# VectorE makes graph messages two units ahead of TensorE's marks in most stages, and adds window sums one unit later

## The chip, the cores and the metric

One core of a Trainium2 chip runs the whole program. The metric is the device time of one execution in microseconds (us). Engines are named as the profile names them: PE is TensorE (PEld its weight loads), DVE is VectorE, ACT is ScalarE, POOL is GpSimd, SP is SyncE.

## The reference, cut to what matters

A graph with 3125 nodes of 256 features and 53125 edges (sorted by destination) goes through two relational graph layers. Beside them the same nodes go through four layers of linear attention and feed-forward, and both results enter a small mixture-of-experts head:

```python
def _mgcn_conv(x, edge_index, edge_type, rel, W_in, W_out, W_loop, b, n):
    m = x[src] * rel[edge_type]
    m = concat([m[:half] @ W_in, m[half:] @ W_out])
    agg = segment_sum(m * norm[dst][:, None], dst)
    return tanh(agg + x @ W_loop + b)
h = emb + res * _mgcn_conv(emb, ..., rel1, ...)
h = h + res * _mgcn_conv(h, ..., rel2, ...)
gnn = h @ mu_w + mu_b
for i in range(4):                       # the mixer, beside it
    x = x + linear_attention(layernorm(x))
    x = x + gelu(layernorm(x) @ W1[i] + b1[i]) @ W2[i] + b2[i]
out = r + experts(layernorm(r))          # r = x_in + gnn + mixer
```

## The kernel before, in words

**The edge work.** Edges are cut into steps of 128; a graph layer has 416 steps. Two steps are a *unit* (`UNIT = 2`), so a graph layer has 208 units, and unit numbers here run from 0 to 415 over both layers. Eight steps are a *window* (`WIN = 8`), so a window is four units (`UW = 4`). For each unit

- POOL gathers the source rows into `xg` (L956, one indirect DMA per step) and, in the first graph layer only, the relation rows of both layers into `rg` (L903, one per step). `xg` has room for 16 steps, that is eight units, so the gather of unit u waits until PE has done unit u-8.
- DVE makes the unit's one-hot matrices (`hot`, L1045) and the messages `xg * rg` (L1054). `hot` has room for eight steps (`HOTS = 8`), so DVE waits before L1045 until PE has done unit u-4. Before L1054 it waits for the unit's gathers (`s_edge`).
- PE multiplies one-hot by messages into a PSUM bank, eight steps (a window) into one of two banks (L2628). PE waits for `s_msg` of the unit, and at the first unit of a window for `s_acc`, which tells that both sums of the window two back have been added.
- DVE adds the window's bank into `acc` twice, for the destination tile and for the next (L1033), each time weighted by `in_tile`. The row number of `acc` is read into a register by `row_numbers` (a `value_load`).

In the second graph layer the relation rows come back from HBM by SP in blocks, so POOL has only the `xg` gathers.

**The order of the work.** Every engine's program is written out by hand. The mixer is cut into stages: a front, then for each layer 0 to 3 a joint (`joint`, the end of the attention) and five feed-forward groups (`iteration`, group (layer, gi)) of five tiles each. A table gives each stage a number of steps: 32 for the front, 14, 14, 14 and 36 for the joints, and (20, 26, 24, 24, 24), (20, 24, 24, 24, 22), (18, 24, 68, 48, 54), (58, 58, 58, 56, 48) for the groups. So group (0,1) begins with unit 33, (0,2) with unit 46, (0,3) with unit 58 and (0,4) with unit 70. Units 0 to 207 end in group (2,2), whose last 20 units run among the tiles of the graph layer's dense update (`dense`). The second graph layer is units 208 to 415, groups (2,3) to (3,4).

Within a stage, `marks` says by which unit each engine has come at each point of the mixer work. PE's program runs `upto(mark)` and then its mixer work. DVE's program has the same marks, but `Edges.stage(at, ahead)` lets it run `ahead` units further at each of them: `upto(k)` makes units while `done < base + k + ahead`, and `one(most)` makes one such unit. `units_ahead` gives that number for the groups: 0 in group (0,0) and in group (2,3), 1 in all others. Joints have `min(lay, 1)`: 0 in joint 0, 1 in the others. The front has 0.

**What stands behind a unit on DVE.** DVE works strictly in program order. In a group with the attention front of the next layer in it, the order after `upto(up0)` is: `f.stats`, which is the layernorm statistics of five rows (L509), `one(up1)`, the means and variances (L516), `one(up1)`, an inverse square root of ten small instructions (L486 to L505) with a third `one(up1)` in it, and then `f.norm(0)` and `f.norm(1)` (L1107), which make the rows that PE transposes next (L545, `f.turn(0)`). Group (0,1) has marks up0 = 2, up1 = 4 and down0 = 5. Further on in a group come `add_ffn` (L1227), `n.add_attention` (L1174), `k_max` (L1114), `n.norm` (L1209) and the softmax work (L1119 to L1160), with `upto` calls between them.

**Where adds stand.** With k the unit within its graph layer, `unit` reads the row numbers of window k//4 - 1 at the start of a unit with k % 4 == 0, and after the message of a unit with k % 4 == 2 or 3 it adds window k//4 - 1 for the first or second time.

Of the kernel before, what the change touches and what calls it, by code (L numbers as in the profile page):

```python
# [45 lines left out]
def build(nc, io, out):  # L46
# [14 lines left out]
    at_joint, at_group, steps = {}, {}, sum(STEPS_FRONT)  # L61
# [9 lines left out]
    RU, UW, BU = RING // UNIT, WIN // UNIT, BLOCK // UNIT  # L71
# [54 lines left out]
    with ExitStack() as ctx:  # L126
# [524 lines left out]
        def dense_before(lay, gi):  # L651
            return (lay, gi) == (DENSE_LAYER, DENSE_GROUP)

        def units_ahead(lay, gi):

            return 0 if (lay, gi) == (0, 0) or dense_before(lay, gi) else 1

        def dense_behind(lay, gi):
            return dense_before(lay, gi + 1)
# [314 lines left out]
        def _(dve):  # L974
# [36 lines left out]
            class Edges:  # L1011
# [24 lines left out]
                def unit(self):  # L1036
                    k, g = self.done, self.g
                    self.done += 1
                    if k % UW == 0 and k:
                        self.row_numbers(k // UW - 1)  # L1040
                    at = k * UNIT
                    s = at % RING
                    hs = at % HOTS
                    dve.wait_ge(s_seg, g * UNITS + (k + 1 + RU - HOTS // UNIT))
                    dve.tensor_tensor(hot[:, hs:hs + UNIT, :], iota_t[:, :].unsqueeze(1).broadcast_to([EP, UNIT, T]),  # L1045
                                      key_tab[:, at:at + UNIT].unsqueeze(2).broadcast_to([EP, UNIT, T]), ALU.is_equal)
                    m, r = xg[:, s:s + UNIT, 0:D], rg[:, s:s + UNIT, 0:D]
                    if g == 0:
                        dve.wait_ge(s_edge[k % RU], (k // RU + 1) * (2 * 16 * UNIT))
                    else:  # L1050
                        dve.wait_ge(s_edge[k % RU], (k // RU + 1 + 2 * (STEPS2 // RING)) * (16 * UNIT))
                        dve.wait_ge(s_r2ld[at // BLOCK % len(s_r2ld)], (at // (2 * RING) + 1) * 16)
                        r = rg2[:, at % (2 * RING):at % (2 * RING) + UNIT, :]
                    dve.tensor_tensor(m, m, r, ALU.mult).then_inc(s_msg, 1)  # L1054
                    if k % UW in (2, 3) and k > UW:
                        self.add(k // UW - 1, k % UW - 2)

                def added(self):

# [958 lines left out]
                front_tiles(fronts[ga], fronts[ga - 1], None if is_last(ga) else fronts[ga + 1], front_marks(ga), upto, one)  # L2018
                at += STEPS_FRONT[ga]
            for lay in range(L):  # L2020
                joint_rest = joint(lay, *edges.stage(at_joint[lay], min(lay, 1)))
                for gi in range(NG):
                    if dense_before(lay, gi):
                        edges = Edges(1)

                    def begin():
                        if lay == L - 1 and gi >= NG - LAST_EARLY:
                            last_norm(gi - (NG - LAST_EARLY))

                    def early():  # L2030

                        if (lay, gi) == (L - 1, NG - 1):
                            edges.flush()

                    def aside(s):
                        if lay == L - 1:
                            dense_beside(gi * (2 * GT) + s)
                            if is_last(gi) and s == GT:
                                logits(0)
                                shift_logits(0)  # L2040
                    if (lay, gi) == (L - 1, 0):
                        general(1, any_unsorted())
                        self_split.read()
                        sums_scaled(0)
                        gate_order()
                    iteration(lay, gi, *edges.stage(at_group[lay, gi], units_ahead(lay, gi)), begin, early, joint_rest, aside)
# [1341 lines left out]
```

## Time and profile before

| | us |
|---|---|
| runs, device time | 1940.79, 1942.41, 1944.38 |
| median | 1942.41 |
| the profiled execution's own time | 1944.52 |
| its span (first to last instruction) | 1942.8 |
| PE busy / DVE busy / POOL busy | 1822.1 / 1248.2 / 1327.5 |

An engine's busy time is the time in which it executes. Idle time before an instruction is put down to what ended it: `<-DMA rg` is the landing of a gather, `<-PE ps_seg` a matmul, `issue` a time in which the engine waited for nothing that the profile shows. The mean granted TensorE clock was 0.991.

### The profile page before, as it was taken

How to read it: one execution, taken by the hardware profiler on the slowest of the kernel's cores; microseconds unless marked ns; L12 is line 12 of the kernel's file. 1: busy time of each engine (PE TensorE's matmuls, PEld its weight loads, DVE VectorE, ACT ScalarE, POOL GpSimd, SP SyncE). 2: the span in 40 equal slices, each digit the busy share in tenths (PEclk: the TensorE clock that was granted, in tenths of full speed). 3: DMA queues.
4: the chain of work that ended last, by engine and by line, in shares of the span. 5: the costliest groups of instructions: out<-in, count | busy, mean ns of one | idle time of the engine just before them, and what ended most of it. 6: DMA issues, size and time to landing. Idle time of an engine off the chain costs nothing.

```text
span 1942.8 us, 28973 instructions
## 1 busy us (share of the span) xinstructions
PE 1822.1 (94%) x9176; PEld 1505.0 (77%) x9176; DVE 1248.2 (64%) x3345; ACT 634.8 (33%) x1552; POOL 1327.5 (68%) x1326
## 2 busy tenths in 40 slices
PE   3889999999899999999999789998999999999999
PEld 1557777887688888768887667886788888888998
DVE  6786465674855576486465555959765666664766
ACT  4452233343323343332333222323122212223443
POOL 6777777777777777777777757777777777770000
PEclk9999999999999999999999999999999999999999
DMA  9568766667866666687777856566767666661000
GB/s 274 178 199 256 205 191 203 187 202 217 250 206 204 194 199 193 208 250 215 206 209 212 263 177 237 181 208 212 236 183 221 201 200 199 190 188 24 15 28 28
DMA packets 194575, 371.44 MB, mean 191 GB/s; under 512 B 37993, under 2 KB 126095, under 8 KB 194430
## 3 DMA queue, kind: packets, MB, share of 16 engines
q0 software_dynamic: 77632, 223.91, 40.4%
q1 hardware_dynamic: 92228, 126.68, 19.8%
q10 hardware_dynamic: 24570, 19.04, 3.4%
q8 instruction: 76, 1.25, 0.3%
q14 instruction: 69, 0.57, 0.1%
HBM read 305.39 MB, written 64.95 MB: 191 GB/s over the span
## 4 chain that ended last, share of the span: by engine, by line
PE 76%; DVE 8%; POOL 5%; issue 4%; DMA 4%; SPq 2%; ACT 1%; DVEq 0%; POOLq 0%; ACTq 0%
PE ps_down L2764 15%; PE ps_hid L2752 15%; PE ps_seg L2628 14%; PE ps_kv L2661 5%; PE ps_x L2716 3%; PE ps_x L545 3%; POOL xg L956 3%; PE ps_kv L3081 2%; PE ps_hid L3228 2%; POOL rg L903 2%; DMA qT_all<-xn_rows 2%; DVE xg L1054 1%; PE ps_hid L2681 1%; PE ps_x L3081 1%; PE ps_hid L3219 1%
## 5 line engine op out<-in xcount | busy, mean ns | idle before, releaser
L956 POOL DMA_INDIRECT xg<-h_rows,idx_tab x416 | 434.3, 1044 | 141.6 <-issue 114.8
L956 POOL DMA_INDIRECT xg<-xn_rows,idx_tab x416 | 434.2, 1044 | 130.9 <-issue 122.2
L903 POOL DMA_INDIRECT rg<-relation_rows,idx_tab x416 | 419.1, 1007 | 133.6 <-issue 126.4
L2628 PE MATMUL ps_seg<-xg,hot 128*125 128x257 f32 x1664 | 417.3, 383 | 18.3 <-DVE xg L1054 18.0
L2752 PE MATMUL ps_hid<-hT,wff 128*128 128x250 f32 (+1 forms) x1920 | 368.1, 340 | 0.2
L2628 PEld LDWEIGHTS ps_seg<-xg,hot 128*125 128x125 f32 x1664 | 307.1, 189 | 74.1 <-DVE xg L1054 15.9
L2764 PE MATMUL ps_down<-wff,gT 128*125 128x256 f32 x1600 | 362.8, 380 | 0.0
L2752 PEld LDWEIGHTS ps_hid<-hT,wff 128*128 128x128 f32 x1920 | 312.7, 189 | 36.9 <-issue 6.8
L2764 PEld LDWEIGHTS ps_down<-wff,gT 128*125 128x125 f32 x1600 | 294.8, 188 | 41.3
L1054 DVE TENSOR_TENSOR xg<-xg,rg 128x512 f32<-128x512 f32 x416 | 285.5, 686 | 61.0 <-DMA rg<-relation_rows,idx_tab 46.1
L2203 ACT ACTIVATE gT<-ps_hid,b1p 128x250 f32<-128x250 f32 (+1 forms) x480 | 177.9, 433 | 292.3 <-PE ps_hid L2752 292.1
L1045 DVE TENSOR_TENSOR hot<-iota_t,key_tab 128x250 f32<-128x250 f32 x416 | 171.2, 411 | 36.8 <-PE ps_seg L2628 26.4
L2661 PE MATMUL ps_kv<-wqkv,hTa 128*125 128x512 f32 x240 | 112.9, 593 | 0.0
L1033 DVE SCALAR_TENSOR_TENSOR acc<-ps_seg,in_tile,acc 125x257 f32 x208 | 99.7, 479 | 17.4 <-PE ps_seg L2628 16.7
L2114 ACT ACTIVATE kx<-ps_kv 125x256 f32<-125x256 f32 x72 | 27.7, 384 | 237.4 <-PE ps_kv L2661 228.5
L1227 DVE TENSOR_TENSOR xres<-xres,ps_down 125x256 f32<-125x256 f32 x100 | 40.0, 416 | 93.9 <-PE ps_down L2764 89.1
L1174 DVE TENSOR_TENSOR xres<-xres,ps_x 125x256 f32<-125x256 f32 x80 | 30.8, 417 | 103.8 <-PE ps_x L2716 103.8
L2189 ACT ACTIVATE hT<-ps_x,ln2p 128x250 f32<-128x250 f32 (+1 forms) x120 | 56.0, 522 | 96.4 <-PE ps_x L545 94.6
L1114 DVE TENSOR_TENSOR kmax<-kmax,kx 125x256 f32<-125x256 f32 x54 | 22.9, 425 | 84.3 <-ACT kx L2114 83.7
L2716 PE MATMUL ps_x<-cwo,qT_all 128*125 128x256 f32 x320 | 76.8, 379 | 0.0
L2661 PEld LDWEIGHTS ps_kv<-wqkv,hTa 128*125 128x125 f32 x240 | 44.7, 187 | 33.2 <-issue 29.0
L2716 PEld LDWEIGHTS ps_x<-cwo,qT_all 128*125 128x125 f32 x320 | 59.8, 187 | 9.3
(373 smaller groups left out, 2390.1 us busy)
## 6 DMA issues: line engine op xcount, KB each, us to landing
second_relation_rows<-rg SPq DMA_DIRECT2D x104, 512.0 KB, 4.0
rg<-second_relation_rows SPq DMA_DIRECT2D x104, 512.0 KB, 4.0
wff<-L_mix_W ACTq DMA_DIRECT2D x8, 1024.0 KB
rg<-relation_rows,idx_tab POOLq DMA_INDIRECT x416, 3.7
xg<-xn_rows,idx_tab POOLq DMA_INDIRECT x416, 3.5
xg<-h_rows,idx_tab POOLq DMA_INDIRECT x416, 3.7
qT_all<-xn_rows SPq DMA_DIRECT2D x25, 112.0 KB
h_rows<-qT_all SPq DMA_DIRECT2D x25, 112.0 KB
```

What stands on the lines that cost most here:

```text
L903: pool.indirect_dma_start(rg[:, k, :], None, rel_d, bass.IndirectOffsetOnAxis(ap=idx_tab[:, step, 1:2], axis=0))\
L956: pool.indirect_dma_start(xg[:, k, 0:D], None, rows, bass.IndirectOffsetOnAxis(ap=idx_tab[:, step, 0:1], axis=0))\
L1033: dve.scalar_tensor_tensor(a, ps_seg[w % 2][0:T, 0:AW], in_tile[:, ds(w, 1), m], a, ALU.mult, ALU.add).then_inc(s_acc, 1)
L1045: dve.tensor_tensor(hot[:, hs:hs + UNIT, :], iota_t[:, :].unsqueeze(1).broadcast_to([EP, UNIT, T]), key_tab[:, at:at + UNIT].unsqueeze(2). ...
L1054: dve.tensor_tensor(m, m, r, ALU.mult).then_inc(s_msg, 1)
L2203: ins = act.activation(out, hidden, ACT.Gelu, bias=b1p[:, ff:ff + 1])
L2628: ins = pe.matmul(ps_seg[u // UW % 2][0:T, 0:AW], hot[:, s % HOTS, :], xg[:, s % RING, :], start=s % WIN == 0, stop=s % WIN == WIN - 1)
L2661: ins = pe.matmul(ps_kv[0:T, :], hTa[:, j % 2, c, :], wqkv[:, c, 0:2 * D], start=c == 0, stop=c == KC - 1)
L2716: ins = pe.matmul(ps_b[j % 2][0:T, :], q[:, c * T:(c + 1) * T], cwo[:, c, :], start=c == 0, stop=c == KC - 1)
L2752: ins = pe.matmul(hidden, w1[:, c, ff * P:(ff + 1) * P], hT[:, a:z, c, :], start=c == 0, stop=c == KC - 1)
L2764: ins = pe.matmul(ps_down[j % 2][0:T, :], gT[:, j % 2, f, :], w2[:, f, :], start=f == 0, stop=f == FC - 1)
L3081: ins = pe.matmul(out_rows, sums(k), weights[k // KC](k % KC), start=k == 0, stop=k == n - 1)
```

## The change

`units_ahead` gives 2 in place of 1, and joints 1 to 3 get 2 in place of 1. Group (0,0), group (2,3), joint 0 and the front stay at 0. In `unit` the reading of row numbers goes behind the message of the unit. The first add of a window follows the message of the unit with k % 4 == 3 (before: 2), and the second follows that of the unit with k % 4 == 0 of the next window (before: 3), ahead of the new row numbers. The last unit of a graph layer does both adds of the window before its own.

```diff
         def units_ahead(lay, gi):
 
-            return 0 if (lay, gi) == (0, 0) or dense_before(lay, gi) else 1
+            return 0 if (lay, gi) == (0, 0) or dense_before(lay, gi) else 2
...
                 def unit(self):
                     k, g = self.done, self.g
                     self.done += 1
-                    if k % UW == 0 and k:
-                        self.row_numbers(k // UW - 1)
                     at = k * UNIT
...
                     dve.tensor_tensor(m, m, r, ALU.mult).then_inc(s_msg, 1)
-                    if k % UW in (2, 3) and k > UW:
-                        self.add(k // UW - 1, k % UW - 2)
+                    if k % UW == 3 and k > UW:
+                        self.add(k // UW - 1, 0)
+                        if k == UNITS - 1:
+                            self.add(k // UW - 1, 1)
+                    if k % UW == 0 and k > UW:
+                        self.add(k // UW - 2, 1)
+                    if k % UW == 0 and k:
+                        self.row_numbers(k // UW - 1)
...
-                joint_rest = joint(lay, *edges.stage(at_joint[lay], min(lay, 1)))
+                joint_rest = joint(lay, *edges.stage(at_joint[lay], 2 * min(lay, 1)))
```

## Rows read from the trace of the kernel before

**Rows 1.** The page: busy us (share of the span) xinstructions.
```profile
PE 1822.1 (94%) x9176; PEld 1505.0 (77%) x9176; DVE 1248.2 (64%) x3345; ACT 634.8 (33%) x1552; POOL 1327.5 (68%) x1326
```
**Rows 2.** Windows: stretch, length, busy us and count by engine, clock, DMA share, GB/s.
```profile
221.00:295.00 74.00, 68.73 (x321) 55.23 (x320) 43.77 (x114) 23.72 (x57) 57.16 (x56) 0.98 0.68 199
...
362.00:428.00 66.00, 65.67 (x319) 53.88 (x318) 40.84 (x109) 25.14 (x58) 50.77 (x51) 1.00 0.67 197
```
**Rows 3.** Waits, whole span: who waited <- for whom: us, times, longest.
```profile
DVE xg L1054 <- DMA rg<-relation_rows,idx_tab: 46.1, 23, 4.5
...
DVE hot L1045 <- PE ps_seg L2628: 26.4, 20, 3.1
...
PE ps_seg L2628 <- DVE xg L1054: 18.0, 16, 2.8
```
**Rows 4.** Waits of PE, 221 to 533 us (groups (0,1) to joint 1).
```profile
PE ps_seg L2628 <- DVE xg L1054: 2.8, 1, 2.8
```
**Rows 5.** Waits of PE, 1230 to 1767 us (second graph layer).
```profile
PE ps_seg L2628 <- DVE xg L1054: 4.9, 5, 1.6
```
**Rows 6.** Waits of POOL, 171 to 498 us (layer 0's groups).
```profile
POOL xg L956 <- PE ps_seg L2628: 0.9, 3, 0.3
```
**Rows 7.** Waits of DVE, 221 to 498 us.
```profile
DVE xg L1054 <- DMA rg<-relation_rows,idx_tab: 44.1, 19, 4.5
```
**Rows 8.** Waits of DVE, 533 to 1050 us (layers 1 and 2), the first of the list.
```profile
DVE kmax L1114 <- ACT kx L2114: 84.8, 20, 7.8
```
**Rows 9.** Timeline, group (0,1): start us, us, instruction, count, [idle before <-releaser].
```profile
230.81 0.69 DVE L1054 TENSOR_TENSOR xg<-xg,rg 128x512 f32<-128x512 f32 x1 [2.46 <-DMA rg<-relation_rows,idx_tab]
...
231.65 1.89 PE L2628 MATMUL ps_seg<-xg,hot 128*125 128x257 f32 x4 [2.77 <-DVE xg L1054]
...
235.93 0.69 DVE L1054 TENSOR_TENSOR xg<-xg,rg 128x512 f32<-128x512 f32 x1 [3.77 <-DMA rg<-relation_rows,idx_tab]
...
238.57 0.75 DVE L1107 TENSOR_SCALAR kx<-xres,mv,rstd 125x256 f32<-125x256 f32 x2
...
239.13 0.41 PE L545 MATMUL ps_x<-ident,kx 125*128 125x125 f32 x2 [1.24 <-DVE kx L1107]
...
242.12 0.69 DVE L1054 TENSOR_TENSOR xg<-xg,rg 128x512 f32<-128x512 f32 x1 [2.47 <-DMA rg<-relation_rows,idx_tab]
```
**Rows 10.** Timeline, late in group (0,3).
```profile
408.60 1.88 POOL L903 DMA_INDIRECT rg<-relation_rows,idx_tab  x1 [0.30 <-issue]
...
412.03 0.95 POOL L903 DMA_INDIRECT rg<-relation_rows,idx_tab  x1 [0.30 <-issue]
...
414.41 0.73 DVE L1209 TENSOR_SCALAR xh<-xres,mv,rstd 125x256 f32<-125x256 f32 x2
...
415.33 0.59 PE L545 MATMUL ps_x<-ident,xh 125*128 125x125 f32 x4
```
**Rows 11.** Timeline, start of group (3,0).
```profile
1376.24 1.13 PE L2628 MATMUL ps_seg<-xg,hot 128*125 128x257 f32 x4 [1.40 <-DVE xg L1054]
...
1389.69 2.07 PE L2628 MATMUL ps_seg<-xg,hot 128*125 128x257 f32 x8 [1.59 <-DVE xg L1054]
```
**Rows 12.** The page's groups: line, operation, count | busy us, mean ns | idle before, releaser.
```profile
L1033 DVE SCALAR_TENSOR_TENSOR acc<-ps_seg,in_tile,acc 125x257 f32 x208 | 99.7, 479 | 17.4 <-PE ps_seg L2628 16.7
```
**Rows 13.** Line 1045's answer: DVE sat idle before it (us, times) until:
```profile
  issue: 7.0, 15
```
**Rows 14.** Timeline of DVE, front, ahead of unit 9.
```profile
100.22 0.42 DVE L1119 TENSOR_REDUCE ktop<-ps_hid 128x2 f32<-128x250 f32 x1 [0.35 <-PE ps_hid L545]
```
**Rows 15.** The page's DMA issues: out<-in, queue, count, us to landing.
```profile
rg<-relation_rows,idx_tab POOLq DMA_INDIRECT x416, 3.7
```
**Rows 16.** Timeline, dense update: unit 207's last gather, unit 206's message, PE later.
```profile
1134.29 0.95 POOL L903 DMA_INDIRECT rg<-relation_rows,idx_tab  x1 [0.30 <-issue]
...
1134.89 0.69 DVE L1054 TENSOR_TENSOR xg<-xg,rg 128x512 f32<-128x512 f32 x1
...
1143.83 0.68 PE L545 MATMUL ps_hid<-ident,qT_all 125*128 125x125 f32 x2 [2.68 <-DMA qT_all<-xn_rows]
```

## The prediction, made before the changed kernel was run

> **What bounds the kernel now.** I began with the page's busy times: PE 94%, POOL 68%, DVE 64% [rows 1]. PE is the bound unless a stage says otherwise. The table of windows says it stage by stage: group (0,3) keeps PE busy 65.67 of 66 us, while the 74 us of group (0,1) have 5.3 us without PE [rows 2]. Then the list of waits: over the whole span PE waits 18.0 us for messages, DVE waits 46.1 us for relation gathers and 26.4 us for a free one-hot slot [rows 3]. So the change can give back some of 18.0 us, and it touches two waits of DVE that are larger. Last, timelines at the places where these waits sit.
>
> Where are the 18.0 us? The front, at 0 ahead before and after, is outside the reach of the new lead. Layer 0's groups and joint 1 hold 2.8 us, in one wait [rows 4]. The second graph layer from 1230 us on holds 4.9 us in five waits [rows 5]. Layers 1 and 2 hold none in their groups. The rest lies in stages that stay at 0.
>
> Where are the gather waits? Of the 46.1 us, 44.1 lie between 221 and 498 us [rows 7]. There POOL is paced by itself: the gaps between its gathers are 0.3 us, nearly all of issue [rows 10], and only 0.9 us in all, three times 0.3, came right after PE's release of a slot [rows 6]. In group (0,3) it issued 51 gathers in 66 us, busy 50.77 us with some 15 us of such gaps [rows 2]. A unit of the first graph layer is four gathers, so it takes about 5.2 us, and a unit of PE takes 66/12 = 5.5 us. Gathers that begin late stay late. In layers 1 and 2 DVE's list of waits begins with 84.8 us for ACT [rows 8] and has no gather in its first seven entries: POOL has caught up.
>
> **The change part by part.** No instruction is added or removed: 416 one-hots, 416 messages and 208 adds stay. No DMA is moved in POOL's or SP's program. What moves is the place in DVE's program at which it waits for a gather or a slot.
>
> *The lead removes PE's waits for messages.* Where PE waits on a message whose gather had long landed, one more unit of lead covers it. That holds for 1376.24 (1.40 us) and 1389.69 (1.59 us) [rows 11] and for three smaller ones, together 4.9 us [rows 5]. I take all of it: **-4.9 us**. Ends: 0, if what is next late on DVE takes each place, and -4.9. The 2.8 us of layer 0 are not among them: the message at 230.81 that PE awaited at 231.65 had itself just waited for its gather [rows 9], and a lead does not make a gather land.
>
> *The lead adds DVE waits for gathers in layer 0, and what stands behind them is due.* The place is the start of group (0,1), where the lead goes from 0 to 2. Before, with 1, `upto(up0)` ends with unit 35, the two `one(up1)` make units 36 and 37 (230.81 and 235.93), both held by their gathers, and then come the inverse square root and the rows `kx` at 238.57, for which PE already waited 1.24 us at 239.13 [rows 9]. With 2, `upto(up0)` ends with unit 36 and the two `one(up1)` make 37 and 38. The message of unit 38 started at 242.12, held by its gather [rows 9], and POOL sends it no sooner. So the last message ahead of `kx` starts at 242.12 in place of 235.93, and `kx` and PE's transpose, which has nothing else to do in its order, come 242.12 - 235.93 = **+6.2 us** later. Ends: +6.2, and 0 if that gather lands 6 us earlier or the lag of that moment is gone; nothing excludes one to two more, see below.
>
> *Does it repeat in (0,2) to (0,4)?* There the rows `xh` at 414.41 are read by PE at 415.33 [rows 10], so a DVE delay of more than about 0.5 us just before would stop PE again, and the DVE waits of 44.1 us over 19 units [rows 7] say that gathers land shortly before DVE wants them. But PE, once 6.2 us later, finds POOL 6.2 us further on, which is more than the 5.5 us of one unit that the new lead asks for. So the loss pays for the lead once: I take 0 more. Ends: 0, and, if each of the three groups paid one more gather wait of the mean size, 3 x 44.1/19 = +7 [rows 7].
>
> *Adds and row numbers in stages at 0 ahead* (front, joint 0, groups (0,0) and (2,3)). PE needs the second add of a window and the message of the same unit; before, the add was done a unit earlier, in idle time of DVE. Now it stands between the unit with k % 4 == 0 and DVE's next work. In the front DVE comes from unit 8 to unit 9 with one idle piece, 0.35 us at 100.22 [rows 14], and the add (0.48 us [rows 12]) and the row numbers (7.0/15 = 0.47 us where they showed as idle time [rows 13]) now fall into that stretch: about 0.95 - 0.35 = +0.6 us each for units 9 and 13. The rest (row numbers no longer ahead of a message) is worth up to -0.4 a window. I take **+1**, ends -1 and +3. In the stages at 2 ahead the adds keep their place relative to PE's marks, so they cost 0.
>
> *The dense update.* Unit 207's message moves into the place of unit 206's, at 1134.89, but its last gather was issued at 1134.29 [rows 16] and lands some 3.7 us later [rows 15], at 1138.0. So DVE stands some 3.1 us in a tile and saves a message and a one-hot in the next. DVE's update feeds the stores and loads of rows, for which PE waits anyway (2.68 us at 1143.83) [rows 16], and part of the 3.1 us is DVE's own idle time in a tile. **+1**, ends 0 and +3.
>
> *The one-hot slots in layer 3.* With a lead of 2 the one-hot of unit u, which waits for PE's unit u-4, is asked for at PE's mark u-2 in place of u-1, so bursts of units end in longer DVE waits. They are 26.4 us in 20 waits now, up to 3.1 us [rows 3], and each may grow by the time of one PE unit, about 1.1 us [rows 11], and by more where other matmuls lie between. DVE is ahead of PE just then, which hides most of it. **+1.5**, ends 0 and +6 (a quarter of the 20 grown waits). Group (2,4), where POOL is again close, gets **+0.5**, ends 0 and +3.
>
> The sum: -4.9 + 6.2 + 1 + 1 + 1.5 + 0.5 = **+5.3 us**. Against the profiled execution's own time of 1944.5 us (span 1942.8) that is 1949.8. This execution lay 2.1 us over the median of 1942.4, so I forecast a median of 1942.4 + 5.3, rounded down because two small terms may be hidden: 1947.5 us.
>
> *A rule that bears on this.* A gather instruction at 408.60, beside two back-to-back units of DVE, took 1.88 us, one at 412.03 took 0.95 us [rows 10]. The Trainium skill, in "GPSIMD Engine Reference", section 1, Specifications, says that POOL's SBUF interface is shared with VectorE and contended when a DVE instruction has two SBUF inputs; the trace agrees, with the 0.93 us between these rows. By that rule the extra unit ahead of the waited-for gather would make +6.2 into up to +7.1; without it, it stays +6.2.
>
> **The rivals.**
>
> *Faster: the lead only covers.* The mechanism is DVE's backlog at the stage starts of the second graph layer (1376.24, 1389.69) [rows 11], and the gathers of layer 0 come early enough that unit 38 isn't waited for. It decides if unit 38's gather lands by the time that DVE had finished unit 37, 236.6 us. For it: runs differ by 3.6 us, and 221 to 295 us is where POOL's lag is decided. Against it: three messages in a row waited 2.5 to 3.8 us for their gathers [rows 9]. The time: -4.9 and the +1 of the adds, and nothing for the rest, 1942.4 - 3.9 = 1938.5 us. The Trainium skill, in "Trainium Kernel Development and Optimization", section Best Practices, advises to double-buffer so that DMA and compute overlap, and a deeper lead is that; by it alone the time would be this one.
>
> *Same: the two cancel.* PE's 6.2 us in group (0,1) shrink to about 4, because the gather wait at 231.65 and the one for `kx` overlap differently, and the 4.9 us are given back. 1942.4 us, from 1939 to 1945. For it: group (0,1) has only 5.3 us without PE now, so its gathers are not far behind. Against it: nothing of PE's work can be drawn ahead of its transpose.
>
> *Slower by more: every group of layer 0 pays.* PE doesn't fall behind POOL for good, because DVE's own waits hold the adds and the next units. Then -4.9 + 6.2 + 7 for the three groups, 1 + 1 + 0.5 as above and 3 for layer 3 make +13.8: 1956.2 us. For it: the slack of about 0.5 us at 414.41 [rows 10]. Against it: POOL in this stretch waits for no slot of PE's [rows 6], so any delay of PE widens POOL's lead.
>
> *The change does nothing there*: DVE already makes each message when its gather lands, so two ahead is one ahead in layer 0. This is true for messages and is why no gain is booked there; it is false for what stands behind them.
>
> **How the numbers follow.** Forecast 0.50, faster rival 0.21, same 0.19, slower by more 0.10. A change of under 0.2% (3.9 us) can't be told from none here. The forecast's own range is +1 to +9 us; of its 0.50 I put 0.40 above 3.9 us and 0.10 below. So slower is 0.40 + 0.10 = 0.50, same is 0.10 + 0.19 = 0.29, faster 0.21 (the faster rival reaches past -3.9 us if most of 4.9 us comes). The range: 1938.0 (the faster rival's time, a little extended; half of that rival lies beyond) to 1954.0 (+11.6, short of the last rival).
>
> **What would show it.** Right: in group (0,1) PE's transpose of `kx` waits about 7 us (1.24 + 6.2) behind a message held by a gather; DVE's waits for relation gathers in (0,2) to (0,4) stay near what they are, with PE's groups still about 66 us; the five waits of PE in the second graph layer go from 4.9 us to under 1; units 9 and 13 in the front wait some 0.6 us longer. Wrong: a group (0,1) that is no longer than 74 us, waits of PE for `xh` or `ktop` in (0,2) to (0,4), or a layer 3 with new waits of PE behind DVE's one-hot waits.

## The result: 1960.2 us, 0.98% slower, and the profile after

The changed kernel takes 1960.16 us (median of 4 runs, 1955.09 to 1964.88), the kernel before beside it 1942.74 us (1940.79 to 1944.38, 4 runs): ratio 1.0098, 95% interval 1.008 to 1.0116 (the plain quotient of the two medians is 1.0090; for all runs below, too, the ratio given is that of the comparison with its interval). I had forecast 1947.5 us with a range to 1954.0. The sign was right, the size was not, and the time lies outside the range. The profiled execution after is the shortest of its four: 1955.09 us, span 1953.4. Against the span before (1942.8) it shows 10.6 us of a loss that is 17.4 us between the medians.

The page of the changed kernel, its first row, against [rows 1]: nobody has more to do.

```profile
PE 1824.2 (93%) x9176; PEld 1506.7 (77%) x9176; DVE 1246.1 (64%) x3345; ACT 635.9 (33%) x1552; POOL 1319.4 (68%) x1326
```

The list of waits of the changed kernel over the whole span (who waited <- for whom: us, times, longest) answers to [rows 3]. Line 1043 is the one-hot (1045 before), 1052 the message (1054 before), 1786 is `mu_added`, the addition of a product to a row in the dense update of layer 3 (1782 before), and 3085 TensorE's next product, which takes that bank.

```profile
DVE hot L1043 <- PE ps_seg L2632: 63.3, 41, 3.6
...
DVE xg L1052 <- DMA xg<-h_rows,idx_tab: 24.4, 20, 4.4
...
DVE xg L1052 <- DMA rg<-relation_rows,idx_tab: 15.3, 8, 4.4
PE ps_seg L2632 <- DVE xg L1052: 8.4, 9, 1.8
PE ps_kv L3085 <- DVE xres L1786: 8.0, 7, 2.5
```

The same wait for `mu_added` in the kernel before:

```profile
PE ps_kv L3081 <- DVE xres L1782: 0.7, 2, 0.4
```

Three things are to be seen. DVE's waits for a one-hot slot went from 26.4 to 63.3 us. PE's waits for messages fell from 18.0 to 8.4 us, which is what a lead does. And a wait of PE that was 0.7 us in two places before, for `mu_added`, is now 8.0 us in seven.

Where the time went, by stages. I took from each timeline the start of the first window matmul of each stage; the columns are the stage's length in us; the dense update is counted from unit 189 to unit 208. (z1, z2 and x9 are experiments of below.)

| stage | before | after | z1 | x9 | z2 |
|---|---|---|---|---|---|
| front, joint 0, group (0,0) | 165.4 | 165.8 | 166.0 | 166.8 | 165.0 |
| group (0,1) | 74.6 | 80.3 | 70.5 | 74.1 | 69.4 |
| groups (0,2) to (0,4) | 202.4 | 200.5 | 199.1 | 200.1 | 200.2 |
| joint 1, layers 1 and 2 up to the dense update | 567.3 | 568.2 | 567.4 | 565.8 | 565.3 |
| dense update | 105.6 | 101.2 | 105.3 | 103.1 | 103.0 |
| group (2,3) | 77.6 | 77.9 | 79.3 | 77.6 | 77.9 |
| group (2,4) | 79.5 | 82.3 | 82.7 | 80.4 | 79.6 |
| joint 3 | 45.9 | 46.1 | 47.8 | 44.4 | 45.0 |
| layer 3 | 392.5 | 399.5 | 400.1 | 413.7 | 393.5 |
| the rest | 176.5 | 176.4 | 176.3 | 176.3 | 176.2 |

The first graph layer (first five rows) ends 0.5 us later than before: in this pair of executions what was lost in group (0,1) was given back. The loss of this execution is group (2,4), +2.8, and layer 3, +7.0.

In layer 3 the waits account for all of it. From its first window matmul to that of unit 415 PE is idle 4.3 us before, 0.65 us of them for `mu_added`; in the changed kernel it is idle 10.4 us, 8.0 of them for `mu_added`; in z1 10.9 and 8.2 us, in z2 4.0 us and none. The growth of this one wait, 7.3 us in the changed kernel and 7.6 in z1, is the growth of the stage, 7.0 and 7.6 us.

**Group (0,1).** Timeline of the changed kernel, against [rows 9] (start us, us, instruction, count, [idle before <-releaser]):

```profile
234.54 0.69 DVE L1052 TENSOR_TENSOR xg<-xg,rg 128x512 f32<-128x512 f32 x1 [2.00 <-DMA rg<-relation_rows,idx_tab]
...
240.28 0.69 DVE L1052 TENSOR_TENSOR xg<-xg,rg 128x512 f32<-128x512 f32 x1 [4.40 <-DMA rg<-relation_rows,idx_tab]
...
242.91 0.76 DVE L1111 TENSOR_SCALAR kx<-xres,mv,rstd 125x256 f32<-125x256 f32 x2
243.47 0.65 PE L545 MATMUL ps_x<-ident,kx 125*128 125x125 f32 x2 [8.32 <-DVE kx L1111]
```

PE's transpose of `kx` waited 8.32 us (1.24 before) behind the message of unit 38, which stood on its gather from 235.9 to 240.3. Windows of the changed kernel (columns as in [rows 2]): the group has 10 us without PE and a granted clock of 0.93, where it had 5.3 us and 0.98; group (0,3) is as it was.

```profile
221.00:295.00 74.00, 64.03 (x292) 51.55 (x291) 39.62 (x107) 22.52 (x54) 56.63 (x58) 0.93 0.68 202
362.00:428.00 66.00, 65.67 (x318) 53.90 (x317) 40.56 (x107) 25.25 (x58) 50.89 (x50) 1.00 0.68 198
```

PE stands 6.0 us later than before at units 46 to 78, 4.0 at unit 82 and 5.4 at unit 182. By the end of the dense update it is gone. The last gather of unit 207 is issued at 1135.92 after and at 1134.29 before [rows 16], and the window matmuls of unit 207 start 0.8 us later than before. What gave it back there is not isolated by a run. In that stretch PE waits for loads of rows (`qT_all`, 15.9 us in the changed kernel, 18.0 before) and for no message before unit 208; it is idle 2.6 us less, and busy 1.8 us less at a clock of 0.97 in place of 0.95. The chain of work that ended last (share of 1065 to 1171 us) runs over POOL's gathers in the changed kernel (38%, 8% over those loads) and over the loads in the kernel before (30%, 4% over POOL's source-row gathers). So POOL's gathers are a bound that a late PE runs into, but they are not seen to hold PE before the change. POOL is not untouched by the late PE, either. Between 55 and 1171 us it waits 17.6 us in 24 for slots of PE's, where it waited 4.3 in 14 before, and its gathers for unit 182 go out 5.4 us later than before; at the last one 1.6 us are left.

```profile
1135.92 0.95 POOL L903 DMA_INDIRECT rg<-relation_rows,idx_tab  x1 [0.30 <-issue]
```

**Start of group (3,0).** The two waits of [rows 11] are gone and a new one stands behind them (timeline of PE, changed kernel):

```profile
1377.50 1.90 PE L2632 MATMUL ps_seg<-xg,hot 128*125 128x257 f32 x8
...
1389.15 1.90 PE L2632 MATMUL ps_seg<-xg,hot 128*125 128x257 f32 x8
1392.71 1.14 PE L2632 MATMUL ps_seg<-xg,hot 128*125 128x257 f32 x4 [1.67 <-DVE xg L1052]
```

**Group (3,3), the largest new wait.** First the kernel before, PE's product and what DVE did ahead of it, from its trace:

```profile
1627.55 0.42 DVE L1045 TENSOR_TENSOR hot<-iota_t,key_tab 128x250 f32<-128x250 f32 x1
...
1633.79 0.42 DVE L1782 TENSOR_TENSOR xres<-xres,ps_kv 125x256 f32<-125x256 f32 x1
...
1634.49 1.99 PE L3081 MATMUL ps_kv<-wqkv,ctxacc 128*125 x8 [0.42 <-DVE xres L1782]
```

Now the same place of the changed kernel:

```profile
1624.95 0.42 DVE L1043 TENSOR_TENSOR hot<-iota_t,key_tab 128x250 f32<-128x250 f32 x1 [1.47 <-PE ps_seg L2632]
...
1628.39 0.42 DVE L1043 TENSOR_TENSOR hot<-iota_t,key_tab 128x250 f32<-128x250 f32 x1 [1.09 <-PE ps_seg L2632]
...
1635.79 0.42 DVE L1043 TENSOR_TENSOR hot<-iota_t,key_tab 128x250 f32<-128x250 f32 x1
...
1641.03 0.69 DVE L1052 TENSOR_TENSOR xg<-xg,rg 128x512 f32<-128x512 f32 x1 [0.32 <-DMA xg<-h_rows,idx_tab]
...
1642.43 0.42 DVE L1786 TENSOR_TENSOR xres<-xres,ps_kv 125x256 f32<-125x256 f32 x1
...
1643.13 1.99 PE L3085 MATMUL ps_kv<-wqkv,ctxacc 128*125 x8 [2.49 <-DVE xres L1786]
```

Read it backwards. PE waits 2.49 us for `mu_added`. Ahead of that stand five units of one-hot and message from 1635.79 on, units 371 to 375; before there were five as well, units 370 to 374 from 1627.55 on. So no unit is added here. One of the five waits 0.32 us for its gather. The rest of the delay stands further ahead. At the start of this piece of work (the feed-forward additions, L1227 at 1614.27 before, L1231 at 1620.23 after) the changed kernel is 6.0 us late; its burst at 1635.79 begins 8.2 us late and its `mu_added` comes 8.6 us late. The 2.2 us between come from the norms of the last rows, which stood behind two one-hots that waited for PE to empty a slot (1.47 us at 1624.95 and 1.09 us at 1628.39; before, the five units ahead of the norms waited for none). A one-hot two units ahead asks for a slot that PE empties one unit later, and its wait stands in DVE's queue ahead of the addition that PE needs next.

Four of the five sessions of experiments below, called the long sessions, ran on three other chips than the fifth, and there every kernel, the one before too, took 2229 to 2326 us at a mean clock of 0.92 to 0.95, with pauses whose end the profile puts down to no instruction (up to 19 us on PE, 25 on DVE, 4 on POOL).

### The profile page after: what moved, and what is told of

Its sections match the earlier page's. It is cut to its first block, busy times and chain, and to the rows that moved or that the text cites. A ratio compares the mean times of both kernels' runs of the same rounds, so it can differ in the third digit from the quotient of the medians.

```text
span 1953.4 us, 28973 instructions
## 1 busy us (share of the span) xinstructions
PE 1824.2 (93%) x9176; PEld 1506.7 (77%) x9176; DVE 1246.1 (64%) x3345; ACT 635.9 (33%) x1552; POOL 1319.4 (68%) x1326
## 4 chain that ended last, share of the span: by engine, by line
PE 76%; DVE 7%; POOL 6%; issue 4%; DMA 3%; SPq 2%; ACT 1%; DVEq 0%; POOLq 0%; ACTq 0%
PE ps_down L2768 16%; PE ps_hid L2756 15%; PE ps_seg L2632 14%; PE ps_kv L2665 5%; POOL xg L956 4%; PE ps_x L2720 3%; PE ps_x L545 3%; PE ps_kv L3085 2%; PE ps_hid L3232 2%; POOL rg L903 2%; DMA xg<-h_rows,idx_tab 1%; PE ps_hid L2685 1%; DVE xg L1052 1%; PE ps_kv L2798 1%; PE ps_hid L3223 1%
## 5 line engine op out<-in xcount | busy, mean ns | idle before, releaser
L956 POOL DMA_INDIRECT xg<-xn_rows,idx_tab x416 | 424.1, 1020 | 141.2 <-issue 119.1
L1043 DVE TENSOR_TENSOR hot<-iota_t,key_tab 128x250 f32<-128x250 f32 x416 | 171.3, 412 | 65.3 <-PE ps_seg L2632 63.3
L1231 DVE TENSOR_TENSOR xres<-xres,ps_down 125x256 f32<-125x256 f32 x100 | 40.0, 416 | 103.8 <-PE ps_down L2768 99.2
L2118 ACT ACTIVATE kx<-ps_kv 125x256 f32<-125x256 f32 x72 | 27.7, 385 | 240.3 <-PE ps_kv L2665 231.0
```

What stands on the lines that cost most here:

```text
L956: pool.indirect_dma_start(xg[:, k, 0:D], None, rows, bass.IndirectOffsetOnAxis(ap=idx_tab[:, step, 0:1], axis=0))\
```

## The experiments

Eighteen runs of twelve kernels, in five sessions. Ratios are against the kernel before in the same session. That of z1, z2, x9 and x5 had it at 1940.13 us (17 runs) and has the narrowest intervals.

### Which part: the lead or the late additions

**x1_adds** (one unit ahead, additions and row numbers as changed) and **x2_lead** (two units ahead, `unit()` as before). x1 against the changed kernel:

```diff
-            return 0 if (lay, gi) == (0, 0) or dense_before(lay, gi) else 2
+            return 0 if (lay, gi) == (0, 0) or dense_before(lay, gi) else 1
-                joint_rest = joint(lay, *edges.stage(at_joint[lay], 2 * min(lay, 1)))
+                joint_rest = joint(lay, *edges.stage(at_joint[lay], min(lay, 1)))
```

x2 keeps these lines of the changed kernel and has row numbers ahead of the unit with k % 4 == 0 and `if k % UW in (2, 3) and k > UW: self.add(k // UW - 1, k % UW - 2)` behind it.

> Lead as before (1 unit), adds and row numbers placed as in the change, in all stages. Theory A (the lead makes DVE wait in its program for gathers and one-hot slots, and what stands behind is due): little moves, +0 to +5 us against before, the part of the adds that I had put at +1 plus what one unit less of room costs at lead 1. Rival B (the late adds hold PE at the first unit of each window): most of the 17 us, +10 us or more, with PE waits behind L1033.

> Lead 2 in the same stages as the change, adds and row numbers placed as before. Theory A: +12 to +18 us against before, PE's wait for kx (L1111 or its like) near 243 us about 8 us, DVE waits for gathers and slots as in the changed kernel. Rival B: +0 to +4 us.

Measured, before at 2249.79: x1 2257.04, ratio 1.0027 (0.9985 to 1.0069); x2 2260.39, 1.004 (0.9998 to 1.0081). Inconclusive: the session doesn't resolve them.

**x3_first, y3_first** (the change in the first graph layer only) and **x4_second, y4_second** (from group (2,4) on only); x and y are the same kernel in two sessions. x4 against the changed kernel (x3 has the complement); where the lead is not 2, additions stand as before:

```diff
-            return 0 if (lay, gi) == (0, 0) or dense_before(lay, gi) else 2
+            return 0 if (lay, gi) == (0, 0) or dense_before(lay, gi) else (1 if lay * NG + gi < 13 else 2)
-                joint_rest = joint(lay, *edges.stage(at_joint[lay], 2 * min(lay, 1)))
+                joint_rest = joint(lay, *edges.stage(at_joint[lay], (0, 1, 1, 2)[lay]))
```

> Lead 2 (with the late adds) only in the stages of the first graph layer, from group (0,1) to (2,2); lead 1 and the old adds from group (2,4) on. Theory A1 (the 6 us lost in group (0,1) are given back in the dense update, whose end is paced by POOL's gathers; the loss that stays is in the second graph layer): -1 to +4 us. Rival A2 (the step in group (0,1) stays to the end, as I predicted): +6 to +10 us.

> Lead 2 (with the late adds) only in the second graph layer: group (2,4), joint 3, layer 3. Theory A1: +9 to +16 us, nearly the whole change. Rival (the sum that I predicted for these stages, -4.9 for covered waits, +1.5 and +0.5): -3 us, that is -5 to 0.

> The kernel of x3_first once more, for the same reason. Theory A1 (the step of 6 us in group (0,1) is given back in the dense update): -1 to +4 us. Rival A2 (it stays): +6 to +10 us. In both, the step of 6 to 7 us is there at the start of group (0,2).

> The kernel of x4_second once more, since the 2250 us of its first comparison leave an interval of 0.8% (before took 1942 elsewhere). Theory A1 (the loss that stays is in the second graph layer): +9 to +16 us. Rival (my predicted sum for these stages): -5 to 0 us.

Measured: first graph layer 1.002 (0.9981 to 1.006) and 0.9969 (0.9925 to 1.0012); second 1.008 (1.004 to 1.0119) and 1.0107 (1.0066 to 1.0147). Twice the change in the second graph layer alone is as slow as the whole change within the error, and in the first it costs nothing that can be told.

**z1_lead_second** (two ahead from group (2,4) on, additions as before everywhere) and **z2_late_second** (one ahead everywhere, additions late in the second graph layer only), in the session with the narrowest intervals. z1 has the two lines of x4 and `unit()` as before; z2 has the two lines of x1 and, in `stage()`:

```diff
+                    late = self.g == 1
```

> Messages two units ahead from group (2,4) to the end of the second graph layer, one unit ahead before it; sums of eight steps and row numbers as in the kernel before, everywhere. Two runs of the same stages with the late additions as well were 0.8% and 1.07% slower than the kernel before. Theory A (the lead alone pays it: DVE's one-hots reach a ring that TensorE has not emptied, and stand there with the norms and additions of the feed-forward groups queued behind them): ratio 1.008 to 1.011, and the waits of the one-hots on the window matmuls sum to over 90 us in the second graph layer. Theory B (the late additions pay it: the second addition of a window comes four units late, and the messages for the next group's attention sum wait for its bank): ratio within 1.003. Theory C (only both together): between, about 1.004.

> One unit ahead everywhere as in the kernel before; only in the second graph layer are the additions and row numbers moved one unit and more further behind, as in the changed kernel. Theory A (lead alone): no difference, ratio within 1.003. Theory B (late additions): 1.008 to 1.011. Theory C (only both together): within 1.004.

Measured, before at 1940.13: z1 1955.64, 1.0084 (1.0063 to 1.0105); z2 1943.66, 1.0016 (1.0002 to 1.0031). The lead pays nearly all of it; the late additions cost 0.4 to 6 us. The waits of z1 in the second graph layer (1230 to 1767 us), where the kernel before has 25.1 us of slot waits in 18:

```profile
DVE hot L1046 <- PE ps_seg L2644: 47.9, 30, 4.0
DVE xg L1055 <- DMA xg<-h_rows,idx_tab: 9.0, 11, 1.8
PE ps_kv L3097 <- DVE xres L1798: 8.2, 7, 2.6
PE ps_seg L2644 <- DVE xg L1055: 2.8, 3, 1.7
```

The slot waits are 47.9 us, not over 90 as I had written. The 8.2 us of PE on `mu_added` (here 1798) are those of the changed kernel; z2 has no such wait in its list. One caution: z2's profiled execution (1932.98 us) is the shortest of its twelve, and its trace alone would have called it 11 us faster.

**x9_layer3** (the change in joint 3 and layer 3 only; lead `2 if lay == 3 else 1`) and **x5_g01_at_1** (the changed kernel, but group (0,1) at one ahead):

```diff
-            return 0 if (lay, gi) == (0, 0) or dense_before(lay, gi) else 2
+            return 0 if (lay, gi) == (0, 0) or dense_before(lay, gi) else (1 if (lay, gi) == (0, 1) else 2)
```

> Two units ahead and late additions in joint 3 and the groups of layer 3 only; group (2,4) and all before it as in the kernel before. If the loss is that of the layer's many groups (a share in each), ratio about 1.007 of the 1.008 to 1.011 of the whole second graph layer, since layer 3 has five of its six stages. If it is paid in group (2,4), where DVE starts a new ring behind the dense update and the gather of its first rows stands ahead, ratio within 1.003.

> The changed kernel with group (0,1) at one unit ahead. The prediction's term: group (0,1) alone costs 6.2 us that stay to the end, so 0.3% faster than the changed kernel, or 1.006 of the kernel before. The other reading, from the changed kernel's trace, in which TensorE is 7.1 us late after that group but only 0.8 us late at the dense update's end, whose pace is set by POOL's gathers: the removal brings nothing at the end, ratio about 1.009 as with the whole change; TensorE's wait for group (0,1)'s keys (8.32 us in the changed kernel) is below 3 us in the profile either way.

Measured: x9 1955.77, 1.0073 (1.0055 to 1.0091): layer 3 with its joint holds it. x5 1958.71, 1.009 (1.0073 to 1.0107), against 1.0098 for the whole change: of the 6.2 us of group (0,1), 0.32%, the two ratios show 0.08%. That they were there and were removed is in x5's timeline:

```profile
235.30 0.41 PE L545 MATMUL ps_x<-ident,kx 125*128 125x125 f32 x2 [2.56 <-DVE kx L1111]
```

2.56 us in place of 8.32. At unit 82 the window matmuls of x5 stand 2.2 us ahead of the kernel before and those of the changed kernel 4.0 us behind it; at unit 207 it is -0.1 and +0.8. Single profiles are no proof of that, since executions of kernels that don't differ from the one before up to there vary as well: at unit 208 z1, z2 and x9 stand 7.3, 11.7 and 5.0 us ahead of it, x5 and the changed kernel 0.3 and 0.5 behind. What counts are the ratios. A loss that stays would give x5 1.0098 - 0.0032 = 1.0066, just outside its interval; but 1.0098 has an error of 0.18% itself, so x5 alone doesn't decide it. z1 and z2 together, with nothing changed in the first graph layer, make 1.0084 + 0.0016 = 1.01, the whole change; and x3 and y3 are at 1.002 and 0.9969. All three speak against a loss that stays in full, and none of them alone is beyond its error by much.

Both profiles also show what the changed kernel's own has not, and what may be a part of why its medians are some 7 us further apart than the spans. Timeline of x9, group (3,4):

```profile
1747.17 0.42 DVE L1046 TENSOR_TENSOR hot<-iota_t,key_tab 128x250 f32<-128x250 f32 x1 [3.06 <-PE ps_seg L2644]
...
1752.12 0.69 DVE L1055 TENSOR_TENSOR xg<-xg,rg 128x512 f32<-128x512 f32 x1 [3.60 <-DMA xg<-h_rows,idx_tab]
...
1753.51 0.42 DVE L1798 TENSOR_TENSOR xres<-xres,ps_kv 125x256 f32<-125x256 f32 x1
...
1754.22 2.95 PE L3097 MATMUL ps_kv<-wqkv,wloop 128*125 x8 [2.78 <-DVE xres L1798]
```

and its windows (columns as in [rows 2]) behind that wait:

```profile
1755.10:1765.30 10.20, 10.20 (x37) 8.88 (x36) 1.38 (x6) 0.68 (x2) 2.00 (x2) 0.50 0.44 69
1754.20:1767.00 12.80, 12.78 (x47) 11.13 (x48) 2.28 (x7) 0.68 (x2) 2.54 (x2) 0.60 0.37 64
1767.00:1775.00 8.00, 8.00 (x57) 7.39 (x56) 4.87 (x12) 2.32 (x7) 0.00 (x0) 1.00 0.00 0
```

A message waits 3.60 us for a gather, PE 2.78 us for the addition behind it, and then the granted clock is 0.60 on the mean of 12.8 us, with 0.50, the level of 1.2 GHz, from 1755.1 to 1765.3, and 1.00, the level of 2.4 GHz, from 1767 on. The same eight matmuls take 2.95 us there, where the clock fell on the way, and 1.89 us in the kernel before. Unit 410, just behind, is 8.0 us later against the kernel before than unit 405 was. In x5 it is 7.6 us. Over the whole of layer 3 PE is busy 398.2 us in x9 and 396.5 in x5 at a mean clock of 0.98, and 388.3 before at 1.00, with the same matmuls: some 10 us of their layer 3, which is 21.2 and 18.8 us longer than before, are clock and not waits. In the changed kernel's own profile and in z1's the same message waits 0.59 and 0.36 us and there is no such step: it hangs on when one gather lands. Two of the four profiles of this kind have it, with executions of 1959.9 and 1966.2 us; the two without it took 1955.1 and 1951.4 us.

### Which of DVE's two waits

**x7_hots_ahead / v7_hots_ahead** (one-hots two ahead, messages one) and **x8_messages_ahead / v8_messages_ahead** (the reverse); both with additions as before. The unit of x7, and in x8 the same with the parts exchanged:

```diff
+                    while self.hots < min(k + 1 + self.more, UNITS):
+                        self.one_hot(self.hots, False)
+                    self.message(k, True)
```

> One-hots two units ahead, messages one unit ahead and adds as before; PE is told of a unit at its message. So DVE's waits for one-hot slots are those of the changed kernel and its waits for gathers those of before. Theory S (slots cause the loss of the second graph layer): +6 to +12 us, with no step in group (0,1). Theory G (gathers cause it): -2 to +3 us.

> Messages two units ahead, one-hots one unit ahead and adds as before; PE is told of a unit at its one-hot. So DVE's waits for gathers are those of the changed kernel and its waits for slots those of before. Theory G: +9 to +17 us, with the step of 6 to 7 us in group (0,1). Theory S: 0 to +4 us, with the step in group (0,1) but no loss after the dense update.

> One-hots two units ahead, messages one unit ahead, additions as in the kernel before. Theory G (what holds VectorE is the gather of a message two units ahead): ratio within 1.003. Theory S (what holds it is the slot of the one-hot, which a ring of four units frees one unit of TensorE later): 1.007 to 1.010. Both in part: between.

> Messages two units ahead, one-hots one unit ahead, additions as in the kernel before. Theory G (the gather of a message two units ahead holds VectorE): ratio 1.007 to 1.010. Theory S (the one-hot's slot): within 1.003. Both in part: between.

Measured: one-hots 1.0016 (0.9982 to 1.005) and 1.0039 (0.9996 to 1.0083); messages 1.0000 (0.9967 to 1.0034) and 0.9996 (0.9954 to 1.0038). Neither alone brings 1.008 to 1.011, but those figures are of x4 and y4, which have late additions and one ahead in the first graph layer. The kernel with both parts two ahead and all else as here is x2, at 1.004 (0.9998 to 1.0081), and from that neither kernel can be told. So these four runs don't separate "gather" from "slot". PE's waits on `mu_added` were 4.5 and 11.2 us with one-hots ahead, 11.3 and 8.0 us with messages ahead, and 25.4 us with both in x2, 16.8 and 14.4 in x4 and y4. With one ahead in layer 3 they were 2.3, 9.2 and 2.6 us (x1, x3, y3). I had expected one of the two parts to carry the loss. What is left open is how much each has in it; what they share is their place in the queue, and that could be moved.

### The place in the queue

**w1_units_behind / u1_units_behind**: z1, but in layer 3 the second of the two units ahead is made behind the row additions of the dense update (`rows_updated`, `mu_added`, `sums_scaled`), not ahead of them. Where the last piece comes (`ctx`), two more steps, `add_b2` and `early`, come ahead of the unit as well. Nothing else differs; each unit is still made two ahead of PE. At each of the five even pieces of a group:

```diff
-                upto(m["up2"])
+                near(m["up2"])
                 aside(2)
+                upto(m["up2"])
```

where `near` is the stage's `upto` with one unit ahead in place of two. **w2_all_behind / u2_all_behind**: the same with two ahead in the first graph layer too.

> As the run with two units ahead in the second graph layer only (additions and row numbers as in the kernel before; 1.0084 of the kernel before), but in layer 3 the last of the two units ahead stands behind the dense update's row additions (rows_updated, mu_added, sums_scaled) and no longer ahead of them. The same one-hots and messages are made, two units ahead of TensorE, with the same waits. Theory A (the loss is the queue order: a message waits on VectorE for its gather or a slot, and the addition behind it, which TensorE's next product waits for, comes late; every wait of TensorE over 0.7 us in layer 3 is on that addition): the waits of TensorE on it, 7.8 us in that run, fall below 2 us, and the ratio comes to 0.999 to 1.003. Theory B (a deeper lead costs by itself, through the one-hot slots or through contention of gathers and VectorE): ratio stays at 1.006 to 1.009.

> As the kernel with units behind the row additions, and two units ahead in the first graph layer as well (additions and row numbers as in the kernel before everywhere). Expected: the same ratio as that kernel, within 0.2%, since the lead of the first graph layer is given back at the dense update; TensorE's wait for the keys of group (0,1) is about 8 us again. If the first layer's lead costs after all, 0.3% more than that kernel.

> A second look at the kernel in which, in layer 3, the last of the two units ahead stands behind the dense update's row additions; the first gave 1.0006 [0.9967, 1.0045] in a session in which every kernel took some 350 us more. Theory A (queue order behind the message): TensorE's waits on the row addition of layer 3, 8.8 us where the unit stands ahead of it, fall below 2 us, ratio 0.999 to 1.003 of the kernel before. Theory B (the deeper lead costs by itself): 1.006 to 1.009.

> A second look at the same with two units ahead in the first graph layer as well; the first gave 0.9839 [0.979, 0.9888] in that session, which nothing in the traces explains. If that gain is real it is below 0.99 here too. Expected by the reading so far: within 0.2% of the kernel above, 0.999 to 1.003, with TensorE's wait for the keys of group (0,1) near 8 us and given back by the end of the dense update.

Measured: w1 1.0006 (0.9967 to 1.0045), u1 1.0004 (0.9961 to 1.0046). With the units ahead of the additions the second graph layer cost 1.008 and 1.0107 in long sessions; z2 puts 0.0016 of that down to the late additions, which w1 and u1 don't have. The differences are 0.7% and 1.0% with errors of some 0.6%. The second pair, x2 and w2/u2, which differ in this order alone, goes the same way: 1.004 against the 0.9839 and 0.9851 below. So the order in the queue looks to be most of the loss, with one reserve: each comparison is between sessions, and z1 itself did not run beside w1. PE's waits on `mu_added` (whole span) are 5.9 and 6.9 us, not below 2 as I had expected, against 16.8 and 14.4 in x4 and y4; in w2 and u2 they are 0.3 and 3.7 us, against 25.4 in x2. The kernels with one ahead there have 2.3 to 9.2 us, so w1 and u1 lie among them. The longest of w1 and of u1, 3.90 and 3.86 us, is not one of the mechanism; u1's timeline shows what stands ahead of it:

```profile
1822.25 0.48 DVE L1033 SCALAR_TENSOR_TENSOR acc<-ps_seg,in_tile,acc 125x257 f32 x1 [3.33 <-remote]
...
1823.05 0.41 DVE L1803 TENSOR_TENSOR xres<-xres,ps_kv 125x256 f32<-125x256 f32 x1
...
1823.75 1.55 PE L3105 MATMUL ps_kv<-wqkv,wloop 128*125 x6 [3.86 <-DVE xres L1803]
```

A pause of 3.33 us whose end the profile puts down to no instruction (`remote`), and no message. In w1 it is such a pause of 3.74 us ahead of a one-hot at 1776.73, whose slot PE had emptied at 1770.56. The wait for `mu_added` goes back to such pauses in these two places.

w2 gave 2247.63 us, 0.9839 (0.979 to 0.9888), and u2 2252.4, 0.9851 (0.98 to 0.9902): 1.5% faster than the kernel before, twice, which I had not expected and can't explain as shown. In their profiles joint 1 with layers 1 and 2 up to the dense update takes 683 and 668 us, in those of w1 and u1 697 us both; x2, with the same lead and additions there, takes 669. So a deeper lead may pay in those layers where engines pause; x3 and y3, also at two ahead there but with late additions, took 708 us both and speak against it. And x2, which is w2 but for the order in layer 3, came out at 1.004 in a session whose kernel before was 38 us faster. Without the pauses the same stages are alike with one ahead and with two (567.3 before, 568.2 after). Whether w2 beats the kernel before in a short session was not run: it is the version that the experiments point to, and its gain was measured in long sessions alone.

## Why the prediction was wrong, by its own steps

| step | forecast | what the runs showed |
|---|---|---|
| lead covers PE's message waits | -4.9 | in the second graph layer they went from 4.9 to 2.0 us: -2.9 (to 2.8 in z1). The two of [rows 11] went; a new one of 1.67 us came at 1392.71, in the same group |
| group (0,1), unit 38's gather holds `kx` | +6.2, to the end | place and size right: PE's wait grew by 7.1 us, the group is 80.3 us long, and 69.4 to 74.6 in the four kernels at one ahead; PE is 6.0 us late behind it. **Wrong that it stays**: 0.8 us are left at unit 207, and x5's ratio is 1.009, not 1.0066 |
| repeat in (0,2) to (0,4) | 0 | right: (0,3) is 66 us with 65.67 of PE, relation waits fell from 46.1 to 15.3 us |
| late additions in stages at 0 ahead | +1 | 0: PE's waits ahead of units 9 and 13 are 0.42 and 0.43 us, 0.40 and 0.41 before; at unit 16 it waits 1.24 us for an addition in place of 1.54 for a message. What late additions do cost (z2: 0.16%) is in the second graph layer, booked at 0 |
| dense update | +1 | its own cost isn't seen apart: 101.2 us in place of 105.6, with PE 4.9 us late at its start; 106.8 us in x5, which came to it no later than the kernel before |
| one-hot slots, layer 3 | +1.5 | **mis-sized**: layer 3 is 7.0 us longer in the changed kernel's profile with the cover above already taken off, and the medians say more: 0.73% = 14 us for joint 3 and layer 3 (x9) |
| group (2,4) | +0.5 | +2.8 in the profile, +3.2 in z1's, where the kernels with one ahead there have 0.1 and 0.9; x9 against z1 puts it at 0.1%, within the error |

**The step that failed is the one-hot slots of layer 3.** With it the terms for the second graph layer, -4.9 + 1.5 + 0.5, made -2.9 us; z1, with the lead there alone, measures +0.84%, 16 us. I had seen that DVE's slot waits would grow: +1.1 us for each of 20 would be 22, they grew by 34.4 us between 1230 and 1767 us (25.1 to 59.5). I then wrote that DVE is ahead of PE, "which hides most of it", and priced it at 1.5 with an end of 6. What I did not do is name what stands behind the waiting instruction in DVE's queue in layer 3, as I had done for `kx` in group (0,1). There it is `mu_added`. The trace of before says how little room it has: of the 23 additions that such a product follows, four end 0.3 us ahead of the product's start, which is the hand-over alone, and behind two of these PE already waits (0.42 us at 1634.49, 0.23 us at 1553.87); the others end 0.7 to 3.6 us ahead. In the changed kernel nine end less than 0.4 us ahead, and PE waits behind seven. I had looked in layer 3 only for waits of PE on messages. Where there is no room, a wait for a slot or a gather ahead of the addition is paid whole; where there are 1 or 2 us, in part. The number of units between two additions is the same as before.

The second error is of the opposite sign. I carried +6.2 us from group (0,1) to the end because "gathers that begin late stay late". It did stay for 800 us, 6.0 us at unit 78 and 5.4 at unit 182, and went in the dense update. Its end there stands behind POOL's last gather, which moved by 1.6 us. My reading is that a delay of PE counts only as far as what the stage hangs on, loads and gathers, is delayed too; the profiles fit it but don't isolate it.

The two errors are of opposite sign and hid each other: without the (0,1) term 1947.5 would have been 1941.3. So the forecast said slower for the wrong reason, and its sign was luck. The "slower by more" rival (1956.2) came closest in time, but with 3 us for layer 3 and 7 more for the groups of layer 0, where it was 14 and 0.

Of the wait of 8.32 us: the Trainium skill, in "GPSIMD Engine Reference", section 1, Specifications, says that the SBUF interfaces of the two are shared, with contention when a DVE instruction has two SBUF inputs; by that the prediction had made +6.2 into up to +7.1. The wait grew by 7.08 us, but this trace does not show that way: the five relation gathers issued between 231 and 242 us took 0.94 to 0.95 us each, and of the four source-row gathers among them one took 1.07 us, as one did in the kernel before.

Shown: the place (second graph layer, then joint 3 with layer 3), the part (the lead), and that in layer 3 of two profiles PE's waits for `mu_added` are the whole growth. Likely, at the edge of the errors: that the first graph layer's loss does not reach the end in full, and that moving one unit behind the row additions removes most of the loss, seen only between long sessions with an error of 0.4% each. Argued from traces, not isolated: what slot and gather each have in it, why the dense update gave the time back, and that the clock's fall behind the late gather makes the 7 us between the profile's loss and the median's.

## What to carry to other kernels

A deeper lead on an in-order engine is a wait moved ahead of everything that stands behind it. For each stage, list what follows the prefetch in the queue and how long ahead of its use it is ready; where that is nothing, every slot or gather wait that is moved ahead of it is paid in full, and the extra unit belongs behind that instruction. Ask also whether a later stage hangs on something else than the bound engine, since that engine's delay may be given back there.

## What was not expected of the hardware

The granted clock of TensorE was 0.60 on the mean of the 12.8 us after a wait of 2.78 us in group (3,4) of x9, and 0.61 in x5 at the same place, in either with some 10 us at the level of 1.2 GHz. So a wait of 2.8 us came with a loss of 8 us in all. A wait of 2.49 us in the changed kernel at 1643.13 was followed by a clock of 1.00. What PE did ahead of the two differs; the runs don't settle what decides.

```profile
1645.00:1652.00 7.00, 7.00 (x37) 6.13 (x36) 2.35 (x6) 0.95 (x3) 5.24 (x6) 1.00 0.55 169
```
